# Dense attention scores with overwritten corners on two alternating bank pairs, and several loads moved, in a macaron transformer layer

## The chip, the cores and the metric

One Trainium2 chip, all 8 cores, one launch. Every core runs the same program on its own 17 token tiles of 128 tokens (16 that it owns and one from its neighbour, which the attention needs as keys and values). Cores 2b and 2b+1 share batch b. The metric is the device time in microseconds of the slowest core.

## The reference, cut to what matters

```python
def attn(x, Wq, Wk, Wv, Wo):           # 16 heads of 128, hidden 2048
    q, k, v = heads(x @ Wq), heads(x @ Wk), heads(x @ Wv)
    bid = arange(S) // 64              # blocks of 64 tokens
    mask = where(abs(bid[:, None] - bid[None, :]) <= 2, 0.0, -1e30)
    p = softmax(q @ k.T * 128 ** -0.5 + mask)
    return merge(p @ v) @ Wo

def ffn(x, U, V, W1, b1, W2, b2):      # 8 low-rank experts of rank 64
    h = relu(x @ W1 + b1)
    alpha = softmax(h @ W2 + b2)
    return einsum('bsk,bskd->bsd', alpha, U @ (V @ x))

x = x + 0.5 * ffn(layernorm(x))
x = x + attn(layernorm(x))
x = x + 0.5 * ffn(layernorm(x))
```

S is 4096, there are 4 batches. A query tile of 128 tokens (two blocks) can see 384 keys, those of its own tile and of the two tiles beside it; of these 384 the first block may not see the last 64, and the second block may not see the first 64.

## The kernel before, in words

The program has four stages: the first feed-forward part ("first"), attention, the output projection ("output"), and the last feed-forward part ("last"). All products are bf16 on TensorE (PE) into PSUM, which has 8 banks: R0 to R4, pL (one bank) and pS (two banks).

**One list per engine.** The kernel is written as one ordered list of operations per engine (class Prog); an operation waits for the semaphores of what it needs. SyncE (SP) issues the stores and all the DMA transposes, GpSimd (POOL) the weight loads. A DMA issued late in SP's list waits for every DMA issued ahead of it to be handed over.

**First stage.** For each token tile: load x, layer norm (statistics on VectorE, DVE; a small power on POOL), and a turned copy xnTa. Tiles 0 to 4 are turned on TensorE (Norm.turn: 16 products with the identity into pS, two copies by ScalarE, ACT), all others by a DMA transpose on SP (Norm.turn_dma); the choice is in ln1_turn. Tiles 5, 6 and 7, ... are worked in blocks: block 1 is tiles 5 and 6 together (items 0 to 15), then tile 7 alone (items 16 to 31). Tile 7 is normalized by ACT after item 11 and turned after item 13. An item is 16 products (L378) and their evict with ReLU by ACT (L385); the small product for the expert weights (L399) of an item comes one item later. The x1 result goes to DRAM (x1d), its layer norm to xn2d. The stage's last block also starts to load xn2d back, turned, as xn2T (load_xn2T: one DMA transpose per tile, on SP), for the token groups 0 to 4.

**Attention.** GROUPS are 6 token groups of 3, 2, 3, 3, 3, 3 tiles. The loop runs over 8 pairs of heads, in each over the 6 groups, and in each over 4 + n pieces: two K pieces and two Q pieces (L715, 16 products of up to 384 columns each), and one V piece for each tile (L705, 16 products of 256 columns). A piece takes the next of four banks in turn (banks4: R0 to R3), so it waits for the evict of the piece four ahead. K and V are evicted by ACT (L722, L709), Q by DVE (L727). Behind each piece stands a slot: between() emits what has been planned for it. A pair has 41 slots.

**Units.** A unit is one query tile of one pair (two heads). Its four steps are planned at slots k, k+1, k+1 and k+7:

- scores (k): four products (L806) of 64 query columns against 320 keys, one for each head and each half of the query tile, that leave the two masked corners of pS out. The corners were filled once with NEG (mask_corners, L884 and L886, in slot 6 of pair 0). Then one maximum over both heads (DVE, L812) and two exponentials with sums (ACT, L815). The next unit's scores wait for the exponentials (S_ended), since all use pS.
- weights (k+1): reciprocal (L822) and two scalings into Pn (DVE, L824).
- turn (k+1): one DMA transpose of Pn into PTs on SP.
- values (k+7): six products (L840; four for tile 0) into bank R4, evicted by DVE (L849) into ost; at the end of a group, ost goes to DRAM (od).

In pair 0 the layer norms of tiles 14 to 16 are still to be done: they stand in DVE's list with three memsets of Pn (L782) in the first slots. Their stores to xn2d, and then load_xn2T of group 5 (tiles 14 to 16), which is first used 30 slots later, are put on SP's list in slots 3 to 6, ahead of the first unit's turn in slot 8.

**Output.** In pair 7 POOL loads the O tiles of group 0 back (early_o, load_o: one transfer of 3 tiles, 1.5 MB) together with one x1 tile (1 MB), at 9 slots after the end of group 1, and those of group 1 (1 MB) at 9 slots after the end of group 2. Then 64 pieces (L974) of 16 products with Wo, on banks4, each added to x by DVE.

**Last.** As the first stage, on all five R banks, pL and pS.

## Time and profile before

| | us |
|---|---|
| median of 3 runs | 1840.62 (1838.12 to 1936.46) |
| the profiled execution's own time | 1838.8 |
| its slowest core (7), first to last instruction | 1837.2 |
| its other cores | 1806.1 to 1823.9 |
| PE busy on core 7 | 1755.8 |
| DVE, ACT busy on core 7 | 746.4, 427.8 |

The profiled execution is one run of the program; its time is that of its slowest core with 1.6 us around it. Engines run beside each other, so a busy time counts only where the end waits for it. Matmuls overlap: the spacing of their starts, not their recorded duration, is what each costs PE.

### The profile page before, as it was taken

Reading aid. Unit: us, or ns where it says so; the run is one execution under the profiler, and the core shown is the slowest. Engines: PE = TensorE matmul, PEld = TensorE weight load, DVE = VectorE, ACT = ScalarE, POOL = GpSimd, SP = SyncE. Lnnn points to the kernel's source line nnn. Section 1 sums busy time; section 2 is a strip of 40 time slices with the busy share of each in tenths; the row PEclk is TensorE's granted clock in tenths of the full one; section 3 lists DMA queues with packets and bytes.
Section 4 is the critical chain, followed back from the end, with each engine's and each line's share of the span. In section 5 each row is a group of like instructions: output and inputs, shape, how many; then the busy total and the mean of one; then the engine's idle time right before and its main releaser. Section 6 shows DMA issues by size and latency. Waiting matters only on the chain.

```text
span 1837.2 us, 34756 instructions; the slowest of 8 cores (1806.1 to 1837.2 us)
## 1 busy us (share of the span) xinstructions
PE 1755.8 (96%) x12964; PEld 1141.5 (62%) x12964; DVE 746.4 (41%) x1389; ACT 427.8 (23%) x1033; POOL 190.8 (10%) x315
## 2 busy tenths in 40 slices
PE   4998999998699999999999999989999999999998
PEld 3866655555377776767677677755444455575556
DVE  4047557525244443444344444434223333153421
ACT  2312321111133333323333333322000111112111
POOL 2001012000011101111101111110000000011000
PEclk9999999999799999999999999999999999999999
DMA  9947456499654545444435445799681583264211
GB/s 210 184 113 218 139 138 178 112 68 227 108 81 67 83 67 82 73 72 76 74 68 80 78 74 78 116 179 220 189 331 47 92 161 126 47 172 127 92 69 47
DMA packets 258134, 218.88 MB, mean 119 GB/s; under 512 B 196400, under 2 KB 234288, under 8 KB 246704
## 3 DMA queue, kind: packets, MB, share of 16 engines
q1 hardware_dynamic: 217136, 121.14, 28.6%
q0 software_dynamic: 38928, 89.70, 27.0%
q10 hardware_dynamic: 1904, 5.81, 1.0%
q8 instruction: 105, 1.72, 0.4%
q14 instruction: 61, 0.50, 0.1%
HBM read 168.93 MB, written 59.24 MB: 124 GB/s over the span
## 4 chain that ended last, share of the span: by engine, by line
PE 86%; SPq 6%; DMA 4%; DVE 2%; ACT 1%; issue 1%; POOL 0%; DVEq 0%; ACTq 0%; POOLq 0%
PE R L715 24%; PE R L378 21%; PE R L705 12%; PE R L974 12%; PE R L430 6%; SPq L102 5%; PE R L462 5%; PE pS L806 3%; PE R L840 2%; DMA W1a<-w 2%; DMA PTs<-Pn 1%; DVE lnb L298 1%; PE pS L282 1%; DMA xnTa<-xna 1%; PE pL L399 0%
## 5 line engine op out<-in xcount | busy, mean ns | idle before, releaser
L378 PE MATMUL R<-xnTa,W1a 128*128 128x384 bf16 (+2 forms) x2048 | 250.7, 283 | 19.9 <-DMA W1a<-w 7.0
L705 PE MATMUL R<-wvS,xn2T 128*128 128x256 bf16 x2176 | 252.1, 273 | 1.6 <-DVE Qb L727 1.6
L715 PE MATMUL R<-xn2T,wkS 128*128 128x384 bf16 (+1 forms) x1536 | 252.9, 318 | 0.0
L715 PE MATMUL R<-xn2T,wqS 128*128 128x384 bf16 (+1 forms) x1536 | 242.8, 312 | 0.0
L815 ACT ACTIVATE Praw<-pS,att 128x384 f32<-128x384 f32 (+1 forms) x256 | 147.1, 575 | 372.5 <-DVE att L812 360.4
L705 PEld LDWEIGHTS R<-wvS,xn2T 128*128 128x128 bf16 x2176 | 209.6, 98 | 35.8 <-issue 9.6
L378 PE MATMUL R<-xnTc,W1c 128*128 128x384 bf16 (+1 forms) x1536 | 228.9, 308 | 0.0
L974 PE MATMUL R<-Wo,Ob 128*128 128x512 bf16 x1024 | 223.5, 380 | 0.0
L378 PEld LDWEIGHTS R<-xnTa,W1a 128*128 128x128 bf16 x2048 | 177.0, 100 | 73.8 <-issue 20.9
L715 PEld LDWEIGHTS R<-xn2T,wkS 128*128 128x128 bf16 x1536 | 146.8, 98 | 88.2 <-issue 11.4
L715 PEld LDWEIGHTS R<-xn2T,wqS 128*128 128x128 bf16 x1536 | 147.8, 99 | 82.5 <-issue 16.0
L378 PEld LDWEIGHTS R<-xnTc,W1c 128*128 128x128 bf16 x1536 | 143.6, 97 | 65.3
L974 PEld LDWEIGHTS R<-Wo,Ob 128*128 128x128 bf16 x1024 | 100.0, 98 | 119.8 <-issue 1.8
L812 DVE TENSOR_REDUCE att<-pS 128x2 f32<-128x768 f32 (+1 forms) x128 | 120.4, 941 | 50.1 <-PE pS L806 30.5
L298 DVE BATCH_NORM_STATS2 lnb<-Xa 128x6 f32<-128x512 f32 x136 | 94.4, 694 | 85.6 <-DMA Xa<-x 70.9
L849 DVE CAST ost<-R 128x256 bf16<-128x256 f32 x128 | 54.4, 425 | 168.4 <-PE R L840 151.9
L824 DVE TENSOR_SCALAR Pn<-Praw,att 128x384 bf16<-128x384 f32 (+1 forms) x256 | 106.5, 416 | 36.5 <-DVE att L822 22.1
L385 ACT ACTIVATE hTa<-R,b1T 128x128 bf16<-128x128 f32 (+2 forms) x128 | 62.4, 488 | 223.0 <-PE pL L399 185.0
L385 ACT ACTIVATE hTc<-R,b1T 128x384 bf16<-128x384 f32 (+1 forms) x96 | 52.4, 546 | 245.4 <-PE pL L399 164.9
L978 DVE TENSOR_TENSOR Xc<-Xc,R 128x512 f32<-128x512 f32 x64 | 44.0, 688 | 159.7 <-PE R L974 153.3
L304 POOL TENSOR_TENSOR lnb<-lnb,mhalf 128x1 f32<-128x1 f32 x50 | 51.1, 1022 | 502.0 <-DVE lnb L303 501.5
L412 DVE TENSOR_TENSOR lgb<-pL,B2b 128x24 f32<-128x24 f32 (+2 forms) x11 | 2.0, 183 | 225.0 <-PE pL L399 225.0
(75 smaller groups left out, 1320.7 us busy)
## 6 DMA issues: line engine op xcount, KB each, us to landing
x1d<-Xa SPq DMA_DIRECT2D x16, 1024.0 KB, 4.0
y<-Xc SPq DMA_DIRECT2D x16, 1024.0 KB, 4.0
Xa<-x POOLq DMA_DIRECT2D x10, 1024.0 KB, 7.2
Xc<-x1d POOLq DMA_DIRECT2D x9, 1024.0 KB, 15.5
xn2d<-xna SPq DMA_DIRECT2D x17, 512.0 KB, 4.1
W1a<-w POOLq DMA_DIRECT2D x16, 512.0 KB, 42.8
Wo<-wo POOLq DMA_DIRECT2D x32, 256.0 KB, 5.4
x2d<-Xc SPq DMA_DIRECT2D x8, 1024.0 KB, 14.1
```

The lines of the kernel that those rows point to most:

```text
L102: self.queue["sync"].append(("op", lambda e: e.dma_start_transpose(dst, src), sem, 16))
L298: p.op("vector", lambda e, j=j: e.bn_stats(st[:, j * 6:j * 6 + 6], x[:, j * 512:(j + 1) * 512]), token, *free)
L378: tok = p.mm(lambda en, c=c: en.matmul(bank[:, 0:w], slot[:, off + c * 128: off + (c + 1) * 128], view(self.xnT, place * D + c * 128, (D, ...
L385: relu = p.op("scalar", lambda en: en.activation(h[:, 0:w], bank[:, 0:w], AF.Relu, bias=b1T[:, e:e + 1]), tok, cst["b1t"], *free)
L430: tok = p.mm(lambda e, c=c, o=o: e.matmul(bank[:, :], self.xnT[:, o:o + 128], self.V[:, c * 512:(c + 1) * 512], start=(c == 0), stop=(c == ...
L462: done = p.mm(lambda e, kc=kc, bank=bank, cg=cg: e.matmul(bank[:, :], zT[:, kc * 128:(kc + 1) * 128], self.U[:, kc * D + cg * 512: kc * D ...
L705: tok = p.mm(lambda e, c=c, o=o: e.matmul(bank[:, 0:256], xn2T[:, o:o + 128], wvS[s][:, c * 256:(c + 1) * 256], start=(c == 0), stop=(c == ...
L715: tok = p.mm(lambda e, c=c: e.matmul(bank[:, 0:w], wS[:, c * 256 + k * 128: c * 256 + (k + 1) * 128], view(xn2T, a * D + c * 128, (D, n), ...
L812: mx = p.op("vector", lambda e: e.reduce_max(a[:, 0:2], view(pS, c0, (512, 2), (1, w)), AX.X, negate=True), tok)
L815: ex = p.op("scalar", lambda e, h=h: e.activation(Praw[b][:, h * 384 + c0:(h + 1) * 384], pS[:, h * 512 + c0: h * 512 + 384], AF.Exp, bias ...
L824: kept["nm"] = p.op("vector", lambda e, h=h: e.tensor_scalar_mul(Pn[u % 3][:, h * 384 + c0:(h + 1) * 384], Praw[b][:, h * 384 + c0:(h + 1) ...
L974: tok = p.mm(lambda e, h=h, o=o: e.matmul(bank[:, :], Ob[:, o:o + 128], Wo[cg][:, h * 512:(h + 1) * 512], start=(h == 0), stop=(h == 15)), ...
```

## The change

Eight banks stay eight, under other names: pX is a tensor of two banks, and R4 and pL are its halves in the feed-forward stages.

- Scores: two products of 128 query columns against 384 keys for a unit (one for each head), all corners computed; then two DVE memsets (one for tile 0) write NEG over the corners of both heads; the maximum and the exponentials as before. Units alternate between pS and pX, so that a unit's scores wait for the exponentials of the unit two ahead. mask_corners goes.
- K, Q, V and Wo pieces run over three banks (R0 to R2), values over R3.
- load_xn2T of group 5 moves from slot 6 of pair 0 to slot 13 (group 2, first piece). The tiles of a group share one semaphore.
- O tiles are loaded one by one (0.5 MB each): tiles 0, 1, 2 at 9, 12 and 15 slots after the end of group 1 of pair 7, the x1 tile at 18, tiles 3 and 4 at 14 and 17 slots after the end of group 2. The later ones are split too, at the places where they were, and each Wo piece waits for its own tile alone.
- Tile 7 is turned on TensorE, not by DMA.

```diff
-    R = [psum(f"R{i}", 512) for i in range(5)]
-    pL = psum("pL", 512)
+    R = [psum(f"R{i}", 512) for i in range(4)]
+    pX = psum("pX", 1024)
     pS = psum("pS", 1024)
+    R.append(pX[:, 0:512])
+    pL = pX[:, 512:1024]
+    Sb = [pS, pX]
...
-        if t < 5:
+        if t < 5 or t == 7:
             xnT_tok[t] = norm.turn(*norm_b[t], xnTa, place[t], free)
...
-    banks4 = Banks(R[:4])
+    banks3 = Banks(R[:3])
...
-    S_ended = [None]
-    O_ended = [banks5.ended[4]]
+    S_ended = [[tbank["ended"][1 - tbank["at"]]], [banks5.ended[4], first.plg_ended]]
+    O_ended = [banks5.ended[3]]
...
         def scores():
+            bank = Sb[b]
             p.wait("tensor", *[kq_end[(pr, g)] for g in range(g_k + 1)], q_end[(pr, GROUP_OF[t])],
-                   S_ended[0])
+                   *S_ended[b])
+            key = (t - 1) * 128 + c0
             for h in range(2):
-                for half in range(2):
-                    lo = max(c0, 64 * half)
-                    hi = 320 + 64 * half
-                    key = (t - 1) * 128 + lo
-                    tok = p.mm(lambda e, h=h, half=half, lo=lo, hi=hi, key=key: e.matmul(
-                        pS[64 * half:64 * half + 64, h * 512 + lo: h * 512 + hi],
-                        Qb[s][:, h * NQ * 128 + t * 128 + 64 * half:
-                              h * NQ * 128 + t * 128 + 64 * half + 64],
-                        Kb[s][:, h * NT * 128 + key: h * NT * 128 + key + hi - lo],
-                        start=True, stop=True), last=(h == 1 and half == 1))
+                tok = p.mm(lambda e, h=h: e.matmul(
+                    bank[:, h * 512 + c0: h * 512 + 384],
+                    Qb[s][:, h * NQ * 128 + t * 128: h * NQ * 128 + (t + 1) * 128],
+                    Kb[s][:, h * NT * 128 + key: h * NT * 128 + key + w],
+                    start=True, stop=True), last=(h == 1))
+            p.op("vector", lambda e: e.memset(
+                bass.AP(bank, 320, [[1024, 64], [512, 2], [1, 64]]), NEG), tok)
+            if j0 == 0:
+                p.op("vector", lambda e: e.memset(
+                    bass.AP(bank, 64 * 1024, [[1024, 64], [512, 2], [1, 64]]), NEG), tok)
             mx = p.op("vector", lambda e: e.reduce_max(
-                a[:, 0:2], view(pS, c0, (512, 2), (1, w)), AX.X, negate=True), tok)
+                a[:, 0:2], view(bank, c0, (512, 2), (1, w)), AX.X, negate=True), tok)
...
-            S_ended[0] = kept["ex"] = ex
+            kept["ex"] = ex
+            S_ended[b] = [ex]
...
-    def load_o(g, eng):
-        a, n = QGROUPS[g]
-        src = bass.AP(od, a * 128 * D, [[D, 128], [128 * D, n], [1, D]])
-        o_tok[g] = p.dma(eng, S(f"lo{g % 2}_{eng}"), view(Ob, (g % 2) * 3 * D, (D, n), (1, D)),
-                         src, o_ended[g % 2], *ost_tok[g])
+    def load_o(t, eng):
+        g = GROUP_OF[t]
+        place = (g % 2) * 3 + t - QGROUPS[g][0]
+        o_tok[t] = p.dma(eng, S(f"lo{place}_{eng}"), Ob[:, place * D:(place + 1) * D], rows(od, t),
+                         o_ended[g % 2], *ost_tok[g])
...
+                if pr == 0 and g == 2 and n == 0:
+                    load_xn2T(5, last_v)
                 if pr == 0 and g == 0:
...
                     if n == 6:
                         ln2_store(16)
-                        mask_corners()
-                        load_xn2T(5, last_v)
                 between()
             next_units(pr, g, slot[0])
             if pr == PAIRS - 1 and g == 1:
-                plan(slot[0] + 9, early_o)
+                for t in range(3):
+                    plan(slot[0] + 9 + 3 * t, call(early_o, t))
+                plan(slot[0] + 18, call(load_x1, 0, "gpsimd", proj_done[(PAIRS - 2, NG - 1)]))
             if pr == PAIRS - 1 and g == 2:
-                plan(slot[0] + 9, lambda: load_o(1, "gpsimd"))
+                for t in (3, 4):
+                    plan(slot[0] + 14 + 3 * (t - 3), call(early_o, t))
```

## Rows read from the trace of the kernel before

**Rows 1.** The page: busy time, share of the span and instructions by engine

```profile
PE 1755.8 (96%) x12964; PEld 1141.5 (62%) x12964; DVE 746.4 (41%) x1389; ACT 427.8 (23%) x1033; POOL 190.8 (10%) x315
```

**Rows 2.** Span and mean granted clock of two cores

```profile
core 3: 1823.9 us, clock 0.990
...
core 7: 1837.2 us, clock 0.989
```

**Rows 3.** Windows of core 7: busy of each engine, PEclk, DMA share, GB/s

```profile
880.00:980.00 100.00, 100.00 (x815) 71.42 (x814) 43.99 (x92) 33.02 (x94) 12.73 (x24) 1.00 0.46 75
```

**Rows 4.** PE's waits on core 7: total us, times, longest us

```profile
PE R L840 <- DMA PTs<-Pn: 26.3, 2, 20.3
```

**Rows 5.** Timeline of PE around one unit's scores: start us, us, what

```profile
800.26 0.50 PE L840 MATMUL R<-PTs,Vb 128*128 128x128 bf16 x6
...
800.69 0.46 PE L806 MATMUL pS<-Kb,Qb 128*64 128x320 bf16 x4
...
801.09 2.77 PE L715 MATMUL R<-xn2T,wqS 128*128 128x384 bf16 x16
```

**Rows 6.** Groups of matmuls by shape: count, busy us, mean ns of one, idle before

```profile
L715 PE MATMUL R<-xn2T,wkS 128*128 128x384 bf16 x1280 | 221.3, 326 | 0.0
...
L840 PE MATMUL R<-PTs,Vb 128*128 128x128 bf16 x752 | 63.4, 220 | 26.3 <-DMA PTs<-Pn 26.3
...
L806 PE MATMUL pS<-Kb,Qb 128*64 128x320 bf16 x480 | 55.8, 312 | 0.0
```

**Rows 7.** Timeline of DVE on core 7, first slots of pair 0

```profile
430.56 0.70 DVE L782 MEMSET Pn<- 128x768 bf16 x1 [0.30 <-DVE Pn L782]
431.43 0.56 DVE L727 TENSOR_SCALAR Qb<-R 128x384 bf16<-128x384 f32 x1 [0.17 <-DVE Pn L782]
...
438.97 0.11 DVE L884 MEMSET pS<- 64x64 f32 x1 [0.22 <-DVE xna L316]
```

**Rows 8.** Timeline of PE on core 7, the same slots

```profile
426.90 3.66 PE L705 MATMUL R<-wvS,xn2T 128*128 128x256 bf16 x32
432.14 1.91 PE L705 MATMUL R<-wvS,xn2T 128*128 128x256 bf16 x16 [1.58 <-DVE Qb L727]
...
440.03 0.41 PE L806 MATMUL pS<-Kb,Qb 128*64 128x192 bf16 x4 [4.23 <-DVE pS L886]
```

**Rows 9.** SP's queue on core 7; time to landing of the last xn2d stores; a piece of the chain

```profile
451.72 3.67 SPq L95 DMA_DIRECT2D xn2d<-xna  x3
459.03 14.69 SPq L102 DMA_TRANSPOSE xn2T<-xn2d  x3
...
xn2d<-xna SPq DMA_DIRECT2D x2, 512.0 KB, 7.9
...
473.81 3.47 DMA PTs<-Pn
```

**Rows 10.** SP's queue on core 3, the same loads

```profile
444.25 15.41 SPq L102 DMA_TRANSPOSE xn2T<-xn2d  x3
```

**Rows 11.** Pair 7 on core 7: one PTs transfer's landing, PE's timeline, a window (PE busy, PEclk)

```profile
PTs<-Pn SPq DMA_TRANSPOSE x1, 17.9
...
1226.28 4.41 PE L715 MATMUL R<-xn2T,wqS 128*128 128x384 bf16 x16
...
1222.80:1229.60 6.80, 4.72 (x21) 0.50 0.93 89
```

**Rows 12.** Timeline of PE on core 7, first stage, block 1, tile 7

```profile
182.67 1.86 PE L378 MATMUL R<-xnTa,W1a 128*128 128x128 bf16 x16 [6.13 <-DMA xnTa<-xna]
...
189.74 1.05 PE L378 MATMUL R<-xnTa,W1a 128*128 128x128 bf16 x16
...
199.72 0.17 PE L399 MATMUL pL<-W2b,hTa 128*128 128x8 bf16 x1 [1.58 <-ACT hTa L385]
```

**Rows 13.** A late evict of a V piece, and the third piece after it

```profile
861.77 0.37 ACT L709 CAST Vb<-R 128x256 bf16<-128x256 f32 x1
...
864.67 1.92 PE L715 MATMUL R<-xn2T,wkS 128*128 128x256 bf16 x16
```

More of the change, by code:

```diff
@@ L193, in view @@
     def view(t, off, *dims):
+        if isinstance(t, bass.AP):
+            off += t.offset
+            t = t.tensor
         return bass.AP(t, off, [[t.ap().ap[0][0], 128], *[list(d) for d in dims]])
@@ L684, in load_xn2T @@
         for t in range(GROUPS[g][0], sum(GROUPS[g])):
-            tok = p.dma_turn(S(f"lxn{t}"), view(xn2T, t * D, (128, 16), (1, 128)), rows(xn2d, t),
-                             xn2_tok[t], *tokens)
-            xn2T_tok.setdefault(g, []).append(tok)
+            xn2T_tok[g] = p.dma_turn(S(f"lxn{g}"), view(xn2T, t * D, (128, 16), (1, 128)),
+                                     rows(xn2d, t), xn2_tok[t], *tokens)
     kq_end = {}
@@ L698, in proj @@
         w = n * 128
-        i, bank, ended = banks4.next()
-        p.wait("tensor", slab_tok[(kind, pr)], *xn2T_tok[g], ended)
+        i, bank, ended = banks3.next()
+        p.wait("tensor", slab_tok[(kind, pr)], xn2T_tok[g], ended)
         if kind == "v":
@@ L729, in proj @@
                 q_end[(pr, g)] = end
-        banks4.ended[i] = end
+        banks3.ended[i] = end
         proj_done[(pr, g)] = tok
@@ L879, in build_nc @@
     ready_after = [(0, 2), (2, 4), (4, 7), (7, 10), (10, 13), (13, 16)]
-    masked = [None]
-    def mask_corners():
-        for h in range(2):
-            p.op("vector", lambda e, h=h: e.memset(pS[0:64, h * 512 + 320: h * 512 + 384], NEG),
-                 *tbank["ended"])
-            masked[0] = p.op("vector", lambda e, h=h: e.memset(
-                pS[64:128, h * 512: h * 512 + 64], NEG), *tbank["ended"])
-        S_ended[0] = masked[0]
     def next_units(pr, g, k):
@@ L968, in wo_piece @@
         g = GROUP_OF[t]
-        i, bank, ended = banks4.next()
-        p.wait("tensor", wo_tok[cg], o_tok[g], ended)
+        i, bank, ended = banks3.next()
+        p.wait("tensor", wo_tok[cg], o_tok[t], ended)
         place = (g % 2) * 3 + t - QGROUPS[g][0]
@@ L1004, in build_nc @@
     load_w1c(0, *attn_end)
-    load_o(2, "scalar")
+    for t in (5, 6, 7):
+        load_o(t, "scalar")
     for t in range(3):
@@ L1010, in build_nc @@
         if t == QGROUPS[g][0] and g > 1:
-            load_o(g + 1, "scalar")
+            for q in range(QGROUPS[g + 1][0], sum(QGROUPS[g + 1])):
+                load_o(q, "scalar")
         for cg in range(4):
@@ L1015, in build_nc @@
             store_x2(t)
-    load_o(5, "scalar")
+    for t in (14, 15):
+        load_o(t, "scalar")
     norm_c = Norm(Pool(xnc))
-    tbank["ended"] = [S_ended[0]] * 2
+    tbank["ended"] = [S_ended[0][0]] * 2
     norm_c_b, xnTc_tok = {}, {}
```

22 lines of the change are left out of this document (10 added, 12 removed).

## The prediction

> **What bounds the kernel now.** I read the page first, then the cores, the windows by stage, PE's waits, and the timelines around each wait. The page has PE busy for 96% of the span and no other engine above half [rows 1]; the windows have it busy for all of a pair of heads in attention, 100.00 of 100 us, with DVE at 44 and ACT at 33 [rows 3]. So PE is the bound, and time can come off in two ways: less PE work in attention, or less waiting. The slowest core is 7 [rows 2]. On it PE waits 26.3 us for turned weights (PTs) in two places, 20.3 and 6.0 [rows 4], 4.2 for the corner memsets [rows 8] and 6.1 for a turned tile 7 in the first stage [rows 12]. With the 1.6 of rows 8 that is 38 us; of the 81.4 us in which PE is not busy (1837.2 - 1755.8) the other 43 lie mostly at the start and the ends, which the change leaves alone.
>
> **Scores.** In rows 5 the last of six values products starts at 800.26 + 0.50 - 0.22 = 800.54 (0.22 is the duration of one, rows 6), and these products start every (0.50 - 0.22)/5 = 0.056 us, so the next work could start at 800.60. The Q piece starts at 801.09. One unit's scores thus take 0.49 us of PE. A product of 384 columns costs (2.77 - 0.33)/15 = 0.163 in a stream [rows 5, 6], so the two dense ones cost 0.325. Saved: 0.16 us x 128 units = 20.5 us, on every core, all on the path, since PE is never idle there. The other end: the four old products lie so close that the last starts 0.46 - 0.31 = 0.15 us after the first [rows 5, 6]; alone in a row 320 columns need 0.133 or more each (the same rate), so the two halves of a head run together, and the streaming is some 0.30 of the 0.49. The other 0.19 is idle time at both ends of the unit. If that belonged to any scores product, the dense unit would cost 0.325 + 0.19 = 0.515, and the edit would lose 3 us. I take 20.5: where full-width products follow each other with other operands nothing is lost (two V pieces of 32 products in 3.66 us, the same 0.109 a product as in one piece, rows 8). Bounds: -3 and +21.
>
> The Trainium skill has a rule that speaks against the edit: TensorEngine Tiling (Array Packing), Overview, says that products of 64 weight columns can run as tiles beside each other, up to twice as fast. By that alone the old form streams 640 columns' worth for 320, and the dense one is slower by 2 x 64 columns, 0.05 us a unit or 7 us. The trace agrees that they overlap (0.15 us between first and last start). The same page, Tiling Modes, Key Properties, says that a change of tiling mode drains the engine; that fits the 0.19 us at the ends.
>
> **Corner memsets.** Two more DVE instructions a unit. One of 64 columns took 0.11 us, one of 768 columns 0.70 [rows 7]; for 128 columns I take 0.16, plus the 0.16 to the next, so 0.64 us for both; bounds 0.5 and 1.7. They lengthen the chain maximum, exponentials, weights, turn. Queued behind it are the Q evicts (DVE) and, behind the exponentials, the K and V evicts (ACT). The cover: the tightest place that repeats is an evict that ends at 862.14 while the third piece on starts at 864.67 [rows 13], 2.5 us of room with three banks; even 1.7 us fits. Their cost is 0. Without the cover it would be 0.64 x 128 = 82 us. The second pair of banks takes away a wait that PE has never met; I put it at 0, between 0 and a small gain.
>
> **Three banks in the first slots of pair 0.** The second V piece could start at 426.90 + 1.75 = 428.65 but now needs the bank of the first Q piece, whose evict stands on DVE behind the Pn memsets and ends at 431.99 [rows 7]. Before, only the third V piece met it, at 432.14 after 1.58 us. So a wait of 3.5 us takes the place of 1.6, and all that follows is 1.75 us later: K ends at 437.4. There, before, the scores waited 4.2 us for the corners, to 440.03 [rows 8]. That wait goes (its DVE place is behind a layer norm that ends at 438.75; the new memsets stand behind it too but PE does not wait for them). Gain 2.6 us on every core.
>
> **Group 5 behind the first turns.** Values of unit 0 were due at 477.41 - 20.27 = 457.1 and waited until 477.4 because on SP's list their turn stood behind the three loads of group 5, 459.03 to 473.7, and then took 3.47 [rows 4, 9]. Now they are due at 457.1 - 2.6 - 0.3 = 454.2, and the turn is issued right behind the xn2d stores, at 455.4. Alone it would land at 459. But the last store, issued near 454.2, lands only 7.9 us later, at 462, and I expect the turn to land behind it, at 463.3. Gain 14.1 us (the 2.6 above included; at best 18). The wait of 9 us is still long enough to bring the clock down, as before. Late next: the group's loads start when its stores have landed, 462.6, take 14.7 again, and unit 2's turn lands 3.5 later, at 480.8. Unit 2's values are due after two Q, three V and one K piece and the units between, 13.9 us, and some 2.2 us of lower clock: 479.4. So 1.4 are given back: net 12.7, bounds 5 and 18. Group 5 itself is used 20 slots later and has cover.
>
> **Pair 7.** The 6.0 us wait is for one PTs transfer that took 17.9 us to land [rows 11] with 1.5 MB of O and 1 MB of x1 issued just ahead. After it a Q piece takes 4.41 in place of 2.77, and the window around it has a granted clock of 0.50, the 1.2 GHz level, with 4.7 us of PE work in it, of which half, 2.3, is lost. The 14.4 us above the usual 3.5 are 5.8 us for each MB. The new loads are 3 slots (some 8 us) apart: 0.5 MB adds 2.9, the x1 tile 5.8. PTs landed 17.9 after issue with 6.0 of wait, so 11.8 are free; 3.5 + 5.8 = 9.3 fits. Gain 8.3 us, bounds 0 and 9. On POOL's list the Wo loads that follow wait less than before; the later split loads on ACT cost 4 more issues there, in a stage where ACT is idle.
>
> **Tile 7.** The wait of 6.13 goes, and the low clock behind it: four items from 182.67 to 189.74 take 7.07 [rows 12] where 64 products at 0.056 take 3.6, so 3.5. Against it: 16 turns on PE, 0.9, and at full clock ACT's normalization of tile 8 shows as a wait of 1.6 (as at 199.72) where it had been partly hidden: 1.1. ACT's two more copies lie in the 3.6 us of two items. Net 7.5 on core 7. Cores without that wait lose up to 1.
>
> **Sum for core 7.** 20.5 + 12.7 + 8.3 + 7.5 = 49.0 us from the profiled execution's own 1838.8: 1790. That execution is 1.8 us below the median of the runs, 0.1%, which I leave. Core 3 (1823.9 + 1.6) is next: it has no tile 7 wait, and its group 5 loads were issued from 444.25 to 459.66 [rows 10]. Its first turn gains some 17 us, and 4 to 6 come back at unit 2, since there PE arrives early: 12 to 13. With 20.5 and some 7 in pair 7 it comes to 1785. So core 7 stays last, with little room: no more than 4 us of a better luck on it would show.
>
> **Rivals.**
> 1. The waits on PTs only change place: SP's list is as long as before, unit 2 stands behind group 5, and in pair 7 the same bytes still share the DMA engines with the turns. For it: the 14.7 us block is 10 us longer than the room of unit 2's turn if PE comes early. Against it: the bytes come 8 us apart. Then 12.7 and 8.3 are lost: 1811.
> 2. The overlapping halves are worth as much as the dense form: scores give -3 in place of 20.5: 1813. For it: the starts of rows 5. Against it: 0.49 against 0.325.
> 3. The first turn does not wait for the store ahead of it and lands at 459, and unit 2 fits: 5 to 6 us more on core 7, then core 3 or another decides: 1782.
> 4. Slower. Memsets into PSUM take far longer than in rows 7, and with three banks the evicts behind the exponentials bind PE. It decides from a chain that is 2.5 us longer [rows 13]. Each us above that is paid at the seam from V to K pieces, 6 in a pair and 48 in all. At 2 us a memset the chain is 4 longer: 1.5 x 48 = 72, and 1790 + 72 = 1862. For it: DVE, once behind, also delays Q. Against it: the same kind of memset took 0.11.
>
> **How the numbers follow.** The forecast 0.68, with a range of its own from 1781 to 1799; rival 1 has 0.12, rival 2 0.07, rival 3 0.09, rival 4 0.04. What a measurement can tell from no change is about 2%, so below 1804 counts as faster. Faster: 0.68 + 0.09, and half of rival 1 where only one of its two waits stays, 0.83. Same: the other half of it and rival 2, 0.13. Slower: 0.04. The range reaches from a little below rival 3 to where rival 1 has lost most: 1776 to 1808.
>
> **What would show it.** Right: scores as two products with 0.33 us from the end of the values products to the next piece; a pair of heads in about 97.4 us in place of 100.1; PE's wait for PTs below 12 us in all with the 6.0 in pair 7 gone; a 3.5 us wait of the second V piece near 429; no wait for xnTa near 180. Wrong: a wait of V or K pieces for ACT within pairs (rival 4), L806 followed by an idle time as before (rival 2), waits on PTs at unit 2 or in the last third of pair 7 (rival 1).

## The result, and the profile after

The changed kernel takes 1814.64 us (median of four runs) against 1840.62 before. Three of the four take 1811.65, 1813.04 and 1816.24 us; in the fourth one die (four of the cores) ran slower and it took 1948, as happens to every kernel now and then, and such runs are left out of all ratios and times from here on. The ratio is 0.986, with a 95% interval from 0.983 to 0.990: 1.0 to 1.8% faster, less than the 2% from which a change counts as faster. Forecast were 1790 us and a range from 1776 to 1808. **The prediction was wrong**: it has about twice the gain that there is.

The page of the changed kernel (it shows core 3, the slowest now), and then spans and clocks of three cores (beside [rows 1] and [rows 2]):

```profile
PE 1736.0 (96%) x12724; PEld 1149.9 (63%) x12724; DVE 787.0 (43%) x1633; ACT 429.8 (24%) x1035; POOL 192.2 (11%) x318
```
```profile
core 0: 1806.9 us, clock 0.991
...
core 3: 1811.4 us, clock 0.989
...
core 7: 1800.1 us, clock 0.993
```

Core 7, the slowest before, is 37.1 us shorter. Core 3 is now last. PE's waits on core 7 and core 3 of the changed kernel, for [rows 4], columns as there:

```profile
core 7 of [0, 1, 2, 3, 4, 5, 6, 7], span 1800.1 us
...
PE R L850 <- DMA PTs<-Pn: 17.2, 4, 7.4
...
PE R L711 <- DVE Qb L733: 3.3, 1, 3.3
```
```profile
core 3 of [0, 1, 2, 3, 4, 5, 6, 7], span 1811.4 us
...
PE R L850 <- DMA PTs<-Pn: 17.1, 4, 6.7
...
PE R L385 <- issue: 9.0, 1, 9.0
```

The wait for xnTa is gone and so is that for the corners; the wait of the second V piece is 3.3 us, where 3.5 were forecast. Yet 17 us of waits for PTs (the turned weights) stand on both. The timeline of PE around a unit, core 3, for [rows 5], and DVE beside it:

```profile
801.04 0.50 PE L850 MATMUL R<-PTs,Vb 128*128 128x128 bf16 x6
801.38 0.49 PE L810 MATMUL pS<-Kb,Qb 128*128 128x384 bf16 x2
801.71 2.76 PE L721 MATMUL R<-xn2T,wqS 128*128 128x384 bf16 x16
...
802.77 0.17 DVE L816 MEMSET pS<- 64x128 f32 x1 [0.23 <-DVE ost L859]
803.11 0.17 DVE L819 MEMSET pS<- 64x128 f32 x1 [0.17 <-DVE pS L816]
803.37 0.96 DVE L821 TENSOR_REDUCE att<-pS 128x2 f32<-128x768 f32 x1
```

From the start of the scores to the next piece it is 0.33 us; before, 0.40 and a longer way in. The starts of single products show it whole: from the last values product to the next piece it was 149 + 3 + 157 + 3 + 232 = 544 ns (the two halves of a head start 3 ns apart) and is 56 + 162 + 162 = 380 ns. These spacings are the same in nearly all of the units that stand between values products and a piece. The 0.16 us a unit of the forecast are there.

**A table by stage.** Each column is the time from the first product of one stage to the first of the next, by PE's timeline, the median of the eight cores (so the columns need not add up to a span). "Pair 0" runs from its first K piece to that of pair 1; "pair 7" to the first Wo piece; "Wo 12" is the first 12 of the Wo pieces.

```
kernel (in the order of the text)  pair 0  pairs 1-6  pair 7  Wo 12  span
before                             109.3   100.1      107.6   45.7   1817.1
changed                            108.6    97.3      111.7   46.3   1800.3
old_o_split                        110.5   100.1      100.1   47.6   1816.7
o_grouped                          101.0    97.3      103.1   44.4   1791.2
o_one_slot                         104.2    97.3      102.9   44.4   1789.3
o_late                             100.2    97.3       97.3   54.6   1787.1
halves                             103.4   100.1      100.1   45.8   1802.9
halves_mem                         104.9   100.1      108.2   48.2   1814.3
dense_nomem                        106.8    97.3       97.3   48.6   1788.8
dense_only                         113.4    98.3      106.3   46.7   1812.5
g5_early                           113.8    97.3      106.6   45.8   1804.8
turn7_dma                          100.7    97.3      109.2   47.2   1800.9
best1                               99.5    97.3      102.7   45.4   1783.0
best2                              102.1    97.3       97.3   44.4   1783.4
```

Pairs 1 to 6 give 2.8 us each, close to the forecast (16 units of 0.16 us, 2.6). Pair 7 gives nothing: over a clean pair it costs 14.4 us (111.7 - 97.3), before 7.5. That is where to look. Core 0 of the changed kernel, PE with its waits, and the queues of SP and POOL in the last third of pair 7 (which starts at 1108.3 on that core):

```profile
1169.81 6.05 SPq L102 DMA_TRANSPOSE PTs<-Pn  x2
...
1175.97 1.83 SPq L95 DMA_DIRECT2D od<-ost  x1
...
1178.65 0.53 POOL L95 DMA_DIRECT2D Wo<-wo  x1 [2.73 <-PE R L721]
1179.17 0.54 POOL L95 DMA_DIRECT2D Ob<-od  x1
1179.69 0.56 POOL L95 DMA_DIRECT2D Xc<-x1d  x1
1180.57 18.02 SPq L102 DMA_TRANSPOSE PTs<-Pn  x2
1187.23 0.80 PE L850 MATMUL R<-PTs,Vb 128*128 128x128 bf16 x6 [6.53 <-DMA PTs<-Pn]
```

The third O tile and the x1 tile, planned three slots apart, stand 0.52 us apart behind a Wo load. An item planned for a slot isn't held until that slot: what POOL has to wait for is only what its semaphores say, and the x1 tile's have long been given. The three O tiles go out 56.6, 63.3 and 70.9 us into the pair, so these are spread by some 7 us, but the x1 tile follows at 71.4: the loads are not all spread as the forecast took them to be.

### The profile page after: what moved, and what is told of

It is laid out like the page before. It is cut to its first block, busy times and chain, and to the rows that moved or that the text cites. A ratio compares the mean times of both kernels' runs of the same rounds, so it can differ in the third digit from the quotient of the medians.

```text
span 1811.4 us, 34807 instructions; the slowest of 8 cores (1794.1 to 1811.4 us)
## 1 busy us (share of the span) xinstructions
PE 1736.0 (96%) x12724; PEld 1149.9 (63%) x12724; DVE 787.0 (43%) x1633; ACT 429.8 (24%) x1035; POOL 192.2 (11%) x318
## 4 chain that ended last, share of the span: by engine, by line
PE 84%; SPq 7%; DMA 4%; DVE 3%; issue 1%; ACT 1%; POOL 0%; DVEq 0%; ACTq 0%; POOLq 0%
PE R L721 23%; PE R L385 17%; PE R L711 12%; PE R L977 12%; SPq L102 6%; PE R L437 5%; PE R L469 4%; PE pX L385 4%; PE R L850 2%; DVE lnb L305 2%; DMA W1a<-w 2%; DMA PTs<-Pn 1%; PE pX L437 1%; PE pX L469 1%; PE pX L810 1%; PE pS L810 1%
## 5 line engine op out<-in xcount | busy, mean ns | idle before, releaser
L711 PEld LDWEIGHTS R<-wvS,xn2T 128*128 128x128 bf16 x2176 | 214.1, 99 | 35.7 <-issue 3.9
L385 PE MATMUL R<-xnTa,W1a 128*128 128x256 bf16 (+2 forms) x1648 | 205.3, 283 | 24.2 <-issue 9.0
L385 PEld LDWEIGHTS R<-xnTa,W1a 128*128 128x128 bf16 x1648 | 141.6, 99 | 69.3 <-issue 25.8
L385 PE MATMUL R<-xnTc,W1c 128*128 128x384 bf16 (+1 forms) x1232 | 185.1, 307 | 0.0
L385 PEld LDWEIGHTS R<-xnTc,W1c 128*128 128x128 bf16 x1232 | 115.1, 97 | 52.1
L824 ACT ACTIVATE Praw<-pX,att 128x384 f32<-128x384 f32 x128 | 74.4, 581 | 237.5 <-DVE att L821 231.5
L834 DVE TENSOR_SCALAR Pn<-Praw,att 128x384 bf16<-128x384 f32 (+1 forms) x256 | 106.6, 417 | 37.6 <-DVE att L832 23.6
L824 ACT ACTIVATE Praw<-pS,att 128x384 f32<-128x384 f32 (+1 forms) x128 | 72.7, 568 | 195.6 <-DVE att L821 189.4
L392 ACT ACTIVATE hTa<-R,b1T 128x384 bf16<-128x384 f32 (+2 forms) x103 | 50.3, 488 | 192.4 <-PE pX L406 154.2
L392 ACT ACTIVATE hTc<-R,b1T 128x384 bf16<-128x384 f32 (+1 forms) x77 | 42.0, 545 | 202.4 <-PE pX L406 132.0
```

Of the source, the lines that this page charges most:

```text
L385: tok = p.mm(lambda en, c=c: en.matmul(bank[:, 0:w], slot[:, off + c * 128: off + (c + 1) * 128], view(self.xnT, place * D + c * 128, (D, ...
L392: relu = p.op("scalar", lambda en: en.activation(h[:, 0:w], bank[:, 0:w], AF.Relu, bias=b1T[:, e:e + 1]), tok, cst["b1t"], *free)
L711: tok = p.mm(lambda e, c=c, o=o: e.matmul(bank[:, 0:256], xn2T[:, o:o + 128], wvS[s][:, c * 256:(c + 1) * 256], start=(c == 0), stop=(c == ...
L824: ex = p.op("scalar", lambda e, h=h: e.activation(Praw[b][:, h * 384 + c0:(h + 1) * 384], bank[:, h * 512 + c0: h * 512 + 384], AF.Exp, bi ...
L834: kept["nm"] = p.op("vector", lambda e, h=h: e.tensor_scalar_mul(Pn[u % 3][:, h * 384 + c0:(h + 1) * 384], Praw[b][:, h * 384 + c0:(h + 1) ...
```

## The experiments

Each is told by its edit, what was on record before it ran, and what came. Two theories of pair 7 were tried first: the split of the O loads does the harm (A), or the longer chain of softmax does (B). Where no interval is given, the time is one run. "Clean" is a pair that takes no longer than pairs 1 to 6 of the same kernel.

**o_grouped**: the old loads of O and x1 in the changed kernel.

```diff
-                for t in range(3):
-                    plan(slot[0] + 9 + 3 * t, call(early_o, t))
-                plan(slot[0] + 18, call(load_x1, 0, "gpsimd", proj_done[(PAIRS - 2, NG - 1)]))
+                plan(slot[0] + 9, early_o)
...
-                for t in (3, 4):
-                    plan(slot[0] + 14 + 3 * (t - 3), call(early_o, t))
+                plan(slot[0] + 9, lambda: load_o(1, "gpsimd"))
```

> The changed kernel with the O and x1 loads of pair 7 as they were before (one 1.5 MB transfer with the x1 tile behind it at 9 slots after group 1, one of 1 MB at 9 slots after group 2). Pair 7, from its first K piece to the first Wo piece, took 107.5 us before (median of the cores) and 111.7 after; a pair without waits takes 97.3 with the new scores. Theory A, the spread loads share the DMA engines with the Wo loads for longer and catch more turns: pair 7 comes to 102 to 106 us, one wait of 4 to 8 us, and the time to 1803 to 1808. Theory B, the longer chain (scores to turn 6.2 us in place of 5.1) leaves too little room, whatever the loads: pair 7 stays at 109 to 114 and the time at 1812 to 1816.

Measured: ratio to before 0.979, from 0.970 to 0.987, of two runs, 1799.65 and 1803.63. Pair 7 is 103.1, as theory A had it, and 8.6 us better than with the split loads (3.5 and 6.1 against the two kernels below that have the same pair 7): in this kernel the split does cost. Theory B as recorded, "whatever the loads", would have left it at 109 to 114.

**o_one_slot**: the tiles one by one, but all planned at slot 9.

```diff
-                    plan(slot[0] + 9 + 3 * t, call(early_o, t))
-                plan(slot[0] + 18, call(load_x1, 0, "gpsimd", proj_done[(PAIRS - 2, NG - 1)]))
+                    plan(slot[0] + 9, call(early_o, t))
+                plan(slot[0] + 9, call(load_x1, 0, "gpsimd", proj_done[(PAIRS - 2, NG - 1)]))
...
-                    plan(slot[0] + 14 + 3 * (t - 3), call(early_o, t))
+                    plan(slot[0] + 9, call(early_o, t))
```

> The changed kernel with the O loads tile by tile, but all three and the x1 tile in one slot, as the grouped ones were, and tiles 3 and 4 in one slot. If it is the spreading that costs (theory A): pair 7 as with the grouped loads, 102 to 106 us. If smaller transfers are themselves slower: 109 to 114.

Measured: 1800.79 us, pair 7 102.9, as grouped. It is the places of the loads that count, not the number of transfers.

**o_late**: three O tiles in the group before the last of pair 7, which brings no new Wo loads, two in the last group, each with a wait on the newest piece so that it can't go ahead; the x1 tile at the end of SP's list for the pair.

```diff
-        load_o(t, "gpsimd")
+        load_o(t, "gpsimd", proj_done[max(proj_done)])
...
-            if pr == PAIRS - 1 and g == 1:
...
+            if pr == PAIRS - 1 and g == 3:
+                for t in range(5):
+                    plan(slot[0] + 1 + 2 * t, call(early_o, t))
...
+    load_x1(0, "sync", proj_done[(PAIRS - 1, 4)])
```

> The changed kernel with the five O tiles loaded at slots 29, 31, 33, 35 and 37 of pair 7, each held back on POOL by the piece just before it, and the x1 tile loaded by SP next to the others at group 5. Between slots 28 and 34 no Wo load is issued. Theory A: the turns find room, pair 7 takes 97.5 to 101 us, and the time is 1796 to 1802, set by the waits of pair 0. Theory B: waits stay, 106 to 112.

Measured: ratio 0.977, from 0.971 to 0.983. Pair 7 is clean on seven of eight cores (97.3 to 97.5, the other 98.8), where theory B had 106 to 112; a window over the whole of it, core 0 (columns as in [rows 3]):

```profile
1090.80:1188.10 97.30, 97.30 (x784) 72.58 (x783) 48.90 (x123) 33.17 (x93) 19.02 (x36) 1.00 0.92 145
```

But some 8 us come back at once, in the first 12 Wo pieces (54.6 in place of 46.3), behind which the late loads stand.

**old_o_split**: the kernel before with only the split loads. It separates A and B.

```diff
-                plan(slot[0] + 9, early_o)
+                for t in range(3):
+                    plan(slot[0] + 9 + 3 * t, call(early_o, t))
+                plan(slot[0] + 18, call(load_x1, 0, "gpsimd", proj_done[(PAIRS - 2, NG - 1)]))
```

> The kernel before with the O and x1 loads of pair 7 split and placed as in the change (and one semaphore for each group's xn2T loads); scores, banks and the short chain are the old ones. Theory A, the spread loads themselves: pair 7 goes from 107.5 us to 112 to 117. Theory B, the longer chain: 101 to 107, since the chain is the old one.

Measured: 1826.96 us. Pair 7 is 100.1 to 100.4 on all eight cores, without a wait. Core 5:

```profile
1127.60:1227.70 100.10, 100.10 (x816) 71.45 (x814) 44.12 (x92) 33.15 (x94) 19.52 (x37) 1.00 0.96 151
```

**Theory A falls as an explanation by itself**: it had 112 to 117. With the old chain the same loads at the same places take away the 7.5 us that pair 7 had lost before, as the prediction had it (theory B's 101 to 107 is missed on the good side). The third O tile and the x1 tile stand 0.6 us apart here too (72.8 and 73.4 us into the pair), so that by itself does no harm either. The harm is in what the loads meet there.

**halves**: the changed kernel with the old scores (two halves of 320 columns) and the corners filled once.

```diff
-                tok = p.mm(lambda e, h=h: e.matmul(
-                    bank[:, h * 512 + c0: h * 512 + 384],
...
+                for half in range(2):
+                    lo = max(c0, 64 * half)
+                    hi = 320 + 64 * half
...
-            p.op("vector", lambda e: e.memset(
-                bass.AP(bank, 320, [[1024, 64], [512, 2], [1, 64]]), NEG), tok)
```

> The changed kernel with the old scores, four products of 64 query columns that leave out corners filled once in each of pS and pX, so no memset in a unit; two pairs of banks, three banks for the pieces, loads as in the change. If the dense form is what took a pair from 100.1 to 97.3 us: 100.1 again, and the idle times around a unit's scores are back. If the second pair of banks or the freed waits did part of it: 97.5 to 99.5. Scores to turn goes back from 6.2 us to 5.1. Pair 7: theory A 112 to 118, since the loads are spread; theory B 101 to 107.

Measured: 1818.91 us, pairs 100.1, pair 7 100.1 to 100.4 on every core, below both forecasts. Everything of the change but the scores is in it, and pair 7 has no wait. Two things differ from the changed kernel still: the products, and the memsets in the chain.

**dense_nomem**: the changed kernel without the corner memsets. It leaves out the masking of the corners.

```diff
-            p.op("vector", lambda e: e.memset(
-                bass.AP(bank, 320, [[1024, 64], [512, 2], [1, 64]]), NEG), tok)
-            if j0 == 0:
-                p.op("vector", lambda e: e.memset(
-                    bass.AP(bank, 64 * 1024, [[1024, 64], [512, 2], [1, 64]]), NEG), tok)
```

> The changed kernel without the corner memsets: the softmax then runs over the dense scores with their corners unmasked, and that part of the mask is left out. Scores to turn goes back from 6.2 us to 5.1. If the longer chain makes the waits of pair 7 with the spread loads: pair 7 falls from 111.7 us to 97.5 to 100. If it is PE's faster pace (97.3 a pair, so 3% more load traffic per us): it stays at 107 to 113. A pair without waits stays at 97.3.

Measured: 1797.12 us, pair 7 97.3 to 98.2. **halves_mem** is the other corner: halves, with the per-unit memsets put back (they write what is there already).

> The kernel with the old scores on two pairs of banks, and the corner memsets in every unit all the same (they write what stands there). Scores to turn 6.2 us, a pair 100.1. Chain: pair 7 rises from 100.1 us to 108 to 115. Pace: it stays at 100.1 to 102.

Measured: 1835.94 us; pair 7 is 108.2, from 100.2 to 115.1. Windows over the whole of pair 7, the longest for halves_mem (core 5), and for halves the same core:

```profile
1131.00:1246.10 115.10, 102.77 (x817) 72.36 (x815) 48.77 (x124) 33.17 (x93) 19.80 (x37) 0.94 0.94 131
```
```profile
1127.80:1227.90 100.10, 100.10 (x816) 71.45 (x814) 44.11 (x92) 33.08 (x93) 19.53 (x37) 1.00 0.86 153
```

The table is full: with the split loads and either form of scores, memsets in the chain make pair 7 8 to 14 us longer on the median core, and without them it is clean. **So neither theory holds as it was recorded; what holds is the two together**: the split loads cost only with the longer chain, and the longer chain costs only with the split loads (with grouped ones pair 7 is 5.8 us over a clean pair, where the old chain had 7.5). A pure matter of pace (dense units arrive sooner) is out, since dense_nomem has the same pace as the changed kernel, 97.3 us a pair. That the memsets do it by the delay, and not in another way, isn't shown: no run delays the chain without them.

The turns show it core by core. The sixth turn of pair 7 (issued 61.5 us into it, in dense_nomem 60.7, with the old scores 62.3) lands after 5.8 to 6.7 us in old_o_split, 6.4 to 7.6 in halves, 6.6 to 9.1 in dense_nomem. The changed kernel's pair 7 was profiled three times (changed, g5_early, turn7_dma), on 24 cores: on 19 of them this turn lands after 13.1 to 19.9 us, on the other 5 after 5.5 to 8.9, and two of those 5 have a clean pair. So the longer chain makes the long landing likely, not certain; halves_mem has it on seven cores of eight (11.6 to 16.6, the eighth 7.0 with pair 7 at 100.2).

Core 0 of dense_nomem can be laid beside core 0 of the changed kernel above. Its POOL issues the same loads at the same times of the pair (71.0 and 71.6 us from its start; changed: 70.9 and 71.4), its SP issues the turns 0.7 to 1.5 us sooner:

```profile
1167.96 5.37 SPq L102 DMA_TRANSPOSE PTs<-Pn  x2
...
1174.79 0.37 SPq L95 DMA_DIRECT2D od<-ost  x1
...
1178.34 0.54 POOL L95 DMA_DIRECT2D Ob<-od  x1
1178.86 0.55 POOL L95 DMA_DIRECT2D Xc<-x1d  x1
1178.89 12.53 SPq L102 DMA_TRANSPOSE PTs<-Pn  x3
1179.54 0.50 PE L845 MATMUL R<-PTs,Vb 128*128 128x128 bf16 x6
1184.54 0.50 PE L845 MATMUL R<-PTs,Vb 128*128 128x128 bf16 x6
1191.98 0.49 PE L845 MATMUL R<-PTs,Vb 128*128 128x128 bf16 x6 [0.52 <-DMA PTs<-Pn]
```

The issues of the two queues in this stretch, first the changed kernel's and then dense_nomem's (engine, count, KB each, median us from issue to landing):

```profile
Xc<-x1d POOLq DMA_DIRECT2D x1, 1024.0 KB, 22.6
od<-ost SPq DMA_DIRECT2D x1, 128.0 KB, 26.2
PTs<-Pn SPq DMA_TRANSPOSE x3, 22.3
```
```profile
Xc<-x1d POOLq DMA_DIRECT2D x1, 1024.0 KB, 12.3
od<-ost SPq DMA_DIRECT2D x1, 128.0 KB, 8.2
PTs<-Pn SPq DMA_TRANSPOSE x3, 10.1
```

And windows of 26 us from about the same point of the pair (66 us in), in the same order:

```profile
1174.00:1200.00 26.00, 14.75 (x86) 8.73 (x84) 6.93 (x17) 4.02 (x12) 2.12 (x4) 0.80 1.20 156
```
```profile
1173.00:1199.00 26.00, 25.48 (x203) 18.29 (x201) 12.00 (x25) 8.42 (x23) 4.58 (x8) 1.00 1.08 207
```

The turns issued at 61.5 and 66.2 us of the pair land after 17.2 and 25.3 us; those issued at 60.7 and 64.7 in dense_nomem after 8.6 and 10.1. In the changed kernel PE stands, the granted clock falls to 0.80 (a share of the window at the 1.2 GHz level), and the DMA engines move fewer bytes, not more (156 against 207 GB/s). So the DMA engines are busy all the while (shares of 1.20 and 1.08) and yet deliver less. Why the delay weighs so much in their queues isn't settled: the runs show that it does on most cores, not which packet stands before which.

**dense_only**: the kernel before with only the dense scores and the memsets, one pair of banks.

```diff
+                tok = p.mm(lambda e, h=h, key=key: e.matmul(
+                    pS[:, h * 512 + c0: h * 512 + 384],
...
+            p.op("vector", lambda e: e.memset(
+                bass.AP(pS, 320, [[1024, 64], [512, 2], [1, 64]]), NEG), tok)
```

> The kernel before with the dense scores and their memsets alone: one pair of score banks, four banks for pieces, old loads, tile 7 by DMA. Pairs take 97.3 us, no wait of scores for the exponentials appears, the first V waits are the old ones (1.6 us before the third V piece). Against the kernel before some 22 us less: 1814 to 1820. A rival says that with one pair of banks the memsets, maximum and exponentials of one unit hold up the next scores: pairs of 98 us or more.

Measured: ratio 0.994, from 0.992 to 0.997, with a median near 1823 us where 1814 to 1820 was expected: the rival in the text on record is what came. PE's waits on core 5, and a window of one pair on core 0:

```profile
PE pS L803 <- ACT Praw L817: 11.5, 10, 2.2
```
```profile
917.00:1015.30 98.30, 97.37 (x783) 72.43 (x782) 49.10 (x123) 33.05 (x94) 12.82 (x24) 1.00 0.50 76
```

A pair takes 98.3 us in place of 97.3. With the longer chain the exponentials of one unit come too late for the scores of the next, about once a pair. The second pair of banks, put at 0, is worth 1.0 us a pair, 8 in all. Its grouped loads in pair 7 cost 8 over a clean pair, about what they cost before.

**g5_early and turn7_dma** measure two other terms of the sum, each by undoing one part.

```diff
-                if pr == 0 and g == 2 and n == 0:
-                    load_xn2T(5, last_v)
...
+                        load_xn2T(5, last_v)
```

> The changed kernel with group 5's three loads put back ahead of the first turn (slot 6 of pair 0), all else as changed. If the place of the loads carries the 12.7 us (prediction's term), pair 0 from its first K piece to the next pair's takes 10 to 18 us longer on the cores whose loads were late before (3, 5, 7: 110 to 125 us in place of 99 to 110), and the time is 1820 to 1828. If what was won on core 7 is only luck from run to run, pair 0 has the same spread as in the changed kernel (99 to 114, median 101 to 109) and the time stays at 1810 to 1816.

```diff
-        if t < 5 or t == 7:
+        if t < 5:
```

> The changed kernel with tile 7 turned by DMA again, all else as changed. If the turn on TensorE carries the 7.5 us that were put down for core 7, one or more cores wait for xnTa near 180 us for 2 to 7 us, and the stage before attention is that much longer on them (up to 3.5 us more by the lower clock); on the others it is up to 1 us shorter. If the old wait was an accident of one core, the first stage is the same within 1 us on all eight.

Measured: g5_early 1811.77 us, turn7_dma 1812.64: each is within the spread of the changed kernel's own runs, so the forecast of 1820 to 1828 for g5_early missed. The stages tell more. Pair 0 takes on the mean of the cores 113.6 us with the early loads (100.4 to 121.3); with the late ones 107.4 in the changed kernel and 103.9 in turn7_dma, together 105.6; o_grouped, o_one_slot and o_late, which are the changed kernel up to pair 7, have means of 103.0, 104.6 and 100.7. So the place of group 5 is worth 8.0 us on the mean core by the first two and some 10 by all five, and a wait as long as the old one is back on one of them. PE's waits on core 0 of g5_early:

```profile
PE R L850 <- DMA PTs<-Pn: 25.9, 2, 20.6
```

In turn7_dma the wait for xnTa is back on all eight cores: 0.7 to 1.3 us on four, 5.5 to 7.6 on the others. Longest on core 7:

```profile
186.60 1.86 PE L385 MATMUL pX<-xnTa,W1a 128*128 128x128 bf16 x16 [7.58 <-DMA xnTa<-xna]
```

That core comes to pair 0 at 420.2 us, 5.6 later than in the changed kernel. Before, such a wait stood on two cores (6.0 and 6.1) and about 1 us on the rest. The block in which tile 7 is worked (from the first L462 or L469 product of the block before to that of its own) tells it without the rest of the stage: 83.9 to 85.4 us on all eight cores of the changed kernel; with the DMA (before and turn7_dma) 83.9 to 86.1 on the ten cores with a short wait and 90.0 to 93.1 on the six with a long one. Which cores get the long one changes with the execution; the change takes it from all.

**best1 and best2**: what the runs had taught. Both load three O tiles at slots of the group before the last of pair 7, which brings no new Wo loads, guarded as in o_late, leave the other five of the first eight to ACT's queue behind the pair, take the x1 tile early in pair 7, and issue group 5's loads four slots later. The edit of best1, and then the one wait by which best2 differs from it:

```diff
-                if pr == 0 and g == 2 and n == 0:
+                if pr == 0 and g == 2 and n == 4:
...
+            if pr == PAIRS - 1 and g == 0:
+                plan(slot[0] + 3, call(load_x1, 0, "gpsimd", proj_done[(PAIRS - 2, NG - 1)]))
+            if pr == PAIRS - 1 and g == 3:
...
+                    plan(slot[0] + 2 * t, call(early_o, t))
...
-    for t in (5, 6, 7):
+    for t in range(3, 8):
```

```diff
-                plan(slot[0] + 3, call(load_x1, 0, "gpsimd", proj_done[(PAIRS - 2, NG - 1)]))
+                plan(slot[0] + 3, lambda: load_x1(0, "gpsimd", proj_done[max(proj_done)]))
```

> The changed kernel with the x1 tile loaded by POOL three slots after group 0 of pair 7 (no Wo load is issued there), the O tiles 0 to 2 at slots 28, 30 and 32, each held back by the piece before it, tiles 3 and 4 loaded with the next group when the last unit is done, and the group 5 loads of pair 0 four pieces later, behind the turns of units 2 and 3. Expected: pair 7 at 97.3 to 98 us, the first 12 Wo pieces at 44 to 46 (with the O loads at 29 to 37 they took 54.6), pair 0 at 98 to 108 with no wait at unit 2, and 1785 to 1794. If the waits only change place again: a sum of pair 7 and the first Wo pieces over 150 us.

> As best1, but the x1 tile of POOL is held back by the piece just before slot 10 of pair 7. In best1 it was issued right behind the last Wo load of group 0, since nothing on POOL's list kept it until its slot, and pair 7 took 102.7 us with a wait for PTs 27 us into it. Expected: pair 7 at 97.3 to 99, and 1783 to 1791. If the place of that load is not what made the wait: 102 to 104 again.

Measured: best1 0.979, from 0.970 to 0.988 (lowest 1793.16); best2 **0.975, from 0.971 to 0.980**, runs of 1790.87, 1791.12, 1793.02 and 1793.65. Pair 7 of best1 (102.7) missed its 97.3 to 98, and three of best2's four runs lie above its 1783 to 1791, by 0.1 to 2.7. In best1 the x1 tile, with nothing to wait for, went out right behind a Wo load and cost 2.7 to 5.1 us some 27 us into pair 7; the guard of best2 takes that away, and six of its cores have a clean pair 7 (97.3 to 97.5; core 0 has 105.3, core 5 107.1). On core 7, its last, nearly all of the waits for PTs that are left stand in the first turn of pair 0:

```profile
core 7 of [0, 1, 2, 3, 4, 5, 6, 7], span 1789.6 us
...
PE R L850 <- DMA PTs<-Pn: 8.4, 2, 7.5
```

It beats the kernel before by 2.5%. Against the changed kernel it wasn't timed side by side; by the two ratios it is some 1% faster (0.975 / 0.986).

## Why the prediction was wrong

**The step that failed** is the one on pair 7: "Gain 8.3 us, bounds 0 and 9". Its sum is a landing of "3.5 + 5.8 = 9.3" us, from the bytes issued just ahead, that "fits" into 11.8 us of room. The room held nearly: from the issue of the sixth turn to the place of its values it is 10.9 us on core 0 of the changed kernel, so 9.3 would still have fitted. The landing did not: 13.1 to 19.9 us on 19 of 24 cores, 18.6 on core 7, and 28.0 for the turn behind it. The bytes were as forecast but for the x1 tile's place, and with the old chain they land the turn after 5.8 to 6.7 us. What the sum lacked is that a turn's landing depends on when it meets the loads and not only on how much is ahead. The forecast let the memsets lengthen the chain, but looked for their cover at V and Q evicts alone: from the scores to the issue of the turn it was 5.1 us on average and is 6.2. Old chain and split loads: 100.1, the gain as forecast. New chain and split loads: 111.7 in the changed kernel's profile, 106.6 and 109.2 in two kernels that don't differ from it there. On core 7 the step is 18.2 us out (115.9 against 108.6 - 8.3 - 2.6 = 97.7).

**Core 7 by its own terms.** Its span fell by 37.1 and was forecast to fall by 49.0. The difference of 11.9 is made up of:

```
stage                       forecast   measured   off by
to the first K of pair 0      409.0      414.6     +5.6   (416.5 - 7.5)
pair 0                        111.8       99.5    -12.3   (127.1 - 2.6 - 12.7)
pairs 1 to 6                  585.5      584.1     -1.4   (600.8 - 6 x 2.56)
pair 7                         97.7      115.9    +18.2
Wo pieces and the end         584.2      586.0     +1.8
```

The prediction put core 3 at 1785; it took 1813 (1811.4 and 1.6). There pair 7 is some 13 us out (110.9, forecast 107.5 - 2.6 - 7), and the stage before attention 14.3 us (first K piece at 424.4, before 410.1), by a stall that is told below.

Point by point:

- **Scores, right.** 0.164 us a unit, where 0.16 stood, 97.3 us a pair, where 97.4 stood. Rival 2 (the halves are worth as much) is out. Both forms in the same surroundings: dense_nomem 97.3, halves 100.1. The ways in and out of the old form's products, 149 and 232 ns where the dense form has 56 and 162, are 93 + 70 = 163 of the 164 ns; the forecast had them as "idle time at both ends" and left open whether the dense form has them too. By the Trainium skill, TensorEngine Tiling (Array Packing), Tiling Modes, Key Properties, a change of tiling mode drains the engine; the trace fits that, with 93 and 70 ns more at the two ends.
- **Memsets: cost 0 for PE, wrong.** One takes 0.17 us as forecast (0.16), and DVE's busy time is up by 40.6 us. Both with their gaps take 0.60 us (802.77 to 803.37), as forecast (0.64), but the start of the maximum is 1.16 us later after the scores than before: the first memset also waits its turn on DVE, above behind an evict of values. V and K pieces have no wait within pairs, so the cover named holds and rival 4 (slower, by the evicts) is out; the cover that fails is that of the turns in pair 7, and with one pair of banks that of the scores too.
- **Second pair of banks: 0, wrong.** 1.0 us a pair once the chain is long.
- **First slots, right.** 3.3 us for 3.5, the corner wait gone. On core 7 the last Q piece of group 1 starts 26.6 us after the first K piece of the pair (441.12), before 29.5 (446.03 in that profile): 3.0 less, of which 0.3 is the scores, so the 2.6 us are there.
- **Group 5, right in kind, wrong in size.** Forecast were 12.7 us for core 7, and pair 0 became 27.6 - 2.6 = 25.0 shorter there; on the mean core it is 8 to 10. Below, core 7's first slots: the turns go out at 441.17, behind the stores, and the values run at 451.88 without a wait. The group's loads stand behind them and unit 2's turn does not wait either. This looks like rival 3, but not by its reason: the first turn lands at 446.98, behind the last store (446.13). What differs from the forecast is that SP issued that store at 436.87, where the forecast had it near 454 as before. It had taken one core's late queue for a constant.

```profile
437.08 0.38 PE L810 MATMUL pS<-Kb,Qb 128*128 128x256 bf16 x2
...
441.17 6.44 SPq L102 DMA_TRANSPOSE PTs<-Pn  x2
...
447.77 13.08 SPq L102 DMA_TRANSPOSE xn2T<-xn2d  x3
...
451.88 0.39 PE L850 MATMUL R<-PTs,Vb 128*128 128x128 bf16 x4
```

But core 0 of the same execution has the wait that the forecast had: its last store lands at 455.47 and the turn behind it at 459.18.

```profile
440.05 3.25 SPq L95 DMA_DIRECT2D xn2d<-xna  x3
443.40 8.38 SPq L102 DMA_TRANSPOSE PTs<-Pn  x2
...
459.31 0.59 PE L850 MATMUL R<-PTs,Vb 128*128 128x128 bf16 x4 [9.20 <-DMA PTs<-Pn]
```

- **Tile 7, right in kind.** The wait of 6.13 is gone on every core. The block of tile 7 takes 85.4 us on core 7 where it took 91.5: 6.1 us, forecast 7.5. Yet the core comes to pair 0 only 2.0 us sooner (414.6 for 416.5), because it reached that block 4.1 us later (its mark in the block before is at 126.0 for 121.9), in a part where the change does nothing but rename banks.
- **The slowest core.** It was core 7 by its own bad luck in two places. The forecast took luck away from it and let no other core have any. Core 3 is last at 1811.4 by a stall of PE in the stage before attention, with the low clock after it (granted clock 0.50 from 399 to 404 us; its first K piece is at 424.4 us where the median core's is at 412.8):

```profile
399.38 1.76 PE L385 MATMUL R<-xnTa,W1a 128*128 128x384 bf16 x5 [9.04 <-issue]
```

The profile gives no releaser for it, in the middle of a piece of 16 products. The DMA packets of the trace do: the queue named "q8 instruction" has no packet on this core from 386 us on until one of 16 KB at 397.06, and PE goes on 2.3 us after that; on core 0, which has no such stall, the packet comes at 382.67. In the eleven profiles of the changed kernel and its variants 14 of 88 cores stall so between 380 and 412 us, for 1.9 to 14.5 us, and 13 of them go on 2.3 to 2.5 us after such a packet starts (in the fourteenth the packet itself took 10.2 us). So PE most likely waits for its own instructions. In the kernel before, old_o_split and dense_only no stall is longer than 1.4 us on any of the 24 cores. Why the packet is late, and whether the change makes it so, isn't shown; SP's transposed load of xn2d takes 31.2 us to land at that time on core 3, but 37.7 on core 0 without a stall.

**Rival 1** (1811, chance 0.12) had the time, but by half its mechanism: the waits of pair 7 stayed and grew, while those of pair 0 became less; that its number fits is in part luck, as the stall shows. best2, which has the change's terms without most of the interaction, runs at 1791 to 1794; that this is near the forecast of 1790 doesn't make the forecast right, since its loads stand elsewhere.

## What to carry to other kernels

Two parts of a change that each cost nothing can cost together: with the old chain the moved loads left pair 7 clean, the longer chain cost no more than the old one while the loads were grouped, and both together made the pair 9 to 14 us longer than a clean one. So when a chain grows, go through every place where its product is transferred, not only the engine behind it. Don't add a landing time up from bytes: the same loads landed the same turn after 6 us and after 19. A planned place on a queue is an order and no time: a load that must come late needs a wait on something late (best2's one wait brings pair 7 from 102.7 to 97.3 us). And on eight cores the last core is the worst of eight draws: price a wait that shows on one core by its spread over all, since mending it lets the next come forward.

## What the runs showed of the hardware

- Turns and plain loads on the same DMA engines: with the split loads the sixth turn of pair 7 lands after 5.8 to 9.1 us on 24 cores without the memsets, and after 13.1 to 19.9 on 19 of 24 cores with the chain some 1 us longer. While the turns are late (core 0) the engines have a DMA share of 1.20 against 1.08 and move a quarter less (156 against 207 GB/s).
- Products of 64 columns of weights in two halves run together (starts 3 ns apart), but a group of them costs 93 ns more on the way in and 70 on the way out, in all the 164 ns by which the dense form is faster.
- A memset of 64x128 f32 into PSUM takes 0.17 us on DVE, one of 64x64 takes 0.11; two of them put 0.8 to 1.2 us into the chain, more than their own 0.60 with gaps (scores to turn: halves 5.1, halves_mem 5.9; dense_nomem 5.2, changed 6.2).
- PE can stand for 2 to 14.5 us near 390 us of the execution, on a core that differs from run to run, with no wait of its own; 13 of 14 such stalls end 2.3 to 2.5 us after a 16 KB packet of the DMA queue "instruction" starts (11 profiles).
